# Vision tower kernel: two loads instead of six issued by ScalarE, and four products as three passes on rounded halves

## What is computed

```python
h = _L0_tok_ref(x, ...)                  # patches @ W_proj.T + b_proj + pos_emb
h = h + _L0_attn_ref(_layernorm(h), ...) # linear attention, 16 heads, feature map elu + 1, running sums
h = h + _L0_ffn_ref(_layernorm(h), ...)  # x @ base_w.T + base_b, plus softmax-gated low-rank experts
h = h + _L1_attn_ref(_layernorm(h), ...) # causal softmax attention, one head of width 256
h = h + _L1_ffn_ref(_layernorm(h), ...)  # sigmoid(xr @ W_r) * (relu(xk @ W_k)**2 @ W_v)
```

```python
result = jnp.einsum('bsd,od->bso', x, base_w) + base_b
logits = jnp.einsum('bsd,ed->bse', x, router_w) + router_b
mid = jnp.einsum('bsd,dr->bsr', x, lora_A)
...
scores = jnp.einsum('bqd,bkd->bqk', Q, K) / jnp.sqrt(jnp.asarray(d, x.dtype))
attn = jax.nn.softmax(scores, axis=-1)
return jnp.einsum('bqk,bkd->bqd', attn, V)
```

## Time and profile before

| | before |
|---|---|
| median of 3 runs | 196.55 us (195.1 to 197.55) |
| the profiled execution: time, span | 195.54 us, 193.5 us |
| PE busy | 178.7 us, 92% |
| PEld busy | 151.4 us, 78% |
| DVE busy | 144.4 us, 75% |
| ACT busy | 85.3 us, 44% |
| POOL busy | 84.3 us, 44% |

### The profile page before, as it was taken

One profiled execution on the slowest core, in us unless ns is written; L12 is line 12 of the kernel. 1 busy time (PEld: TensorE's weight loads), 2 busy tenths in 40 slices (PEclk: granted clock), 3 DMA queues, 4 the chain that ended last, 5 costly groups with the idle time before them and its releaser, 6 DMA issues.

```text
span 193.5 us, 4709 instructions
## 1 busy us (share of the span) xinstructions
PE 178.7 (92%) x1676; PEld 151.4 (78%) x1676; DVE 144.4 (75%) x471; ACT 85.3 (44%) x247; POOL 84.3 (44%) x144
## 2 busy tenths in 40 slices
...
GB/s 155 272 250 265 276 310 101 5 5 0 0 3 0 0 3 2 3 23 3 0 23 0 28 5 0 23 3 0 0 28 0 26 23 0 3 0 25 0 23 38
DMA packets 17201, 9.31 MB, mean 48 GB/s; under 512 B 11840, under 2 KB 17180, under 8 KB 17180
## 3 DMA queue, kind: packets, MB, share of 16 engines
...
q10 hardware_dynamic: 1448, 0.95, 1.8%
...
## 4 chain that ended last, share of the span: by engine, by line
PE 77%; SPq 9%; DVE 4%; ACT 2%; issue 2%; DMA 2%; POOL 1%; POOLq 0%; DVEq 0%; ACTq 0%
PE single L653 10%; PE quad L529 8%; PE single L529 7%; PE single L671 6%; PE single L738 5%; PE single L743 5%; PE quad L630 5%; PE single L700 5%; PE single L703 5%; PE single L644 5%; PE single L559 4%; SPq L314 4%; SPq L329 3%; PE single L727 3%; PE single L712 3%; PE single L688 3%
## 5 line engine op out<-in xcount | busy, mean ns | idle before, releaser
L429 POOL TENSOR_TENSOR ln_rs<-ln_ve,mhalf 108x1 f32<-108x1 f32 (+1 forms) x44 | 24.1, 549 | 50.2 <-DVE ln_ve L985 50.1
L1081 DVE TENSOR_TENSOR S<-quad,mask 108x864 f32<-108x864 f32 (+1 forms) x22 | 21.9, 1024 | 0.6 <-PE quad L630 0.6
L529 PE MATMUL single<-wp_hi,x_hi 128*108 128x256 f32 (+1 forms) x66 | 19.3, 293 | 2.0 <-DVE x_lo L939 2.0
L997 DVE TENSOR_SCALAR xn_back<-hB,ln_mv,ln_rs 108x256 f32<-108x256 f32 (+1 forms) x33 | 13.6, 412 | 7.4 <-POOL ln_rs L429 7.1
L529 PE MATMUL single<-wp_hi,x_lo 128*108 128x256 f32 (+1 forms) x66 | 18.5, 280 | 0.0
L529 PE MATMUL single<-wp_lo,x_hi 128*108 128x256 f32 (+1 forms) x66 | 18.5, 280 | 0.0
L442 POOL TENSOR_TENSOR x_lo<-xT,x_hi 128x648 fp32r<-128x648 f32 (+1 forms) x8 | 12.1, 1516 | 5.7 <-ACT x_hi L766 5.7
L457 POOL TENSOR_TENSOR hbb<-hB,baseb 108x256 f32<-108x256 f32 (+1 forms) x11 | 8.3, 753 | 14.2 <-DVE hB L1103 14.2
L971 DVE BATCH_NORM_STATS2 ln_st<-hB 108x6 f32<-108x256 f32 (+1 forms) x33 | 13.8, 422 | 0.3
L480 POOL TENSOR_TENSOR gated<-gated,hB 108x256 f32<-108x256 f32 (+1 forms) x11 | 8.4, 761 | 12.5 <-DVE gated L1183 12.5
L529 PEld LDWEIGHTS single<-wp_hi,x_hi 128*108 128x108 f32 (+1 forms) x66 | 11.2, 169 | 2.6 <-DVE wp_lo L934 2.1
...
## 6 DMA issues: line engine op xcount, KB each, us to landing
...
```

The source lines that it names most:

```text
L429: nc.gpsimd.tensor_tensor(L.rs[0:t, j:j + 1], L.ve[0:t, j:j + 1], mhalf[0:t, :], ALU.pow).then_inc(L.rstd_done, 1)
L529: ins = nc.tensor.matmul(out_ap, lhs, rhs, start=(start and n == 0), stop=(stop and n == len(terms) - 1))
L997: nc.vector.tensor_scalar(L.xn[0:t, j, :], h[0:t, i, :], L.mv[0:t, i, 0:1], L.rs[0:t, i:i + 1], ALU.subtract, ALU.mult).then_inc(L.xn_done, 1)
L1081: nc.vector.tensor_tensor(S[0:t, j, 2 * h:2 * h + 2, 0:4 * t].rearrange("p r (e t) -> p r e t", e=4), quad[0:t, 2 * h:2 * h + 2, 0:4 * t]. ...
```

## The change

1. ScalarE issues the two large loads only; the three of `pos` and the row of `b_proj` go to SyncE's queue, ahead of the three attention weights. `bv` and `bo` get semaphores of their own. `L1_attn_Vw` is loaded earlier, behind `cat` and ahead of units 6 and 7 of x.
2. The products of `ffn`, of `atv` (both) and of `sc` become `product3` on rounded halves. So the turned tokens are kept as `xn_hi` and `xn_lo`, `at` as `at_hi` and `at_lo`, and `wcat`, `G` and `L1_attn_Vw` as halves too. The new VectorE steps are `lo1`, `lo2` (one subtraction for each unit and norm), `lo3` (`at_low`, one for each unit), `late` (two for the weights) and `foldl`; the new ScalarE steps are `cat` and `vwh`.
3. Norm 1 is applied by ScalarE instead of VectorE (`VLN` is (2, 3)), with the GpSimd product `nb`.
4. `GROUPS` is [0,1], [2,3,4], [5,6,7], [8,9,10].
5. Buffers are shared: `kmin`, `qmin` with `kcum`, `qk`; `sm`, `probT` with `xr`; `gated` with `v1`; raw `wcat` and Vw with `S`; some small ones.
6. All five orders (but SyncE's own) and the banks are new. `router` now stands behind `hF.4` and `kf.0`.

The diff, without the order and bank tables and cut to what is told above:

```diff
-GROUPS = [[0, 1, 2], [3, 4, 5], [6, 7, 8], [9, 10]]
+GROUPS = [[0, 1], [2, 3, 4], [5, 6, 7], [8, 9, 10]]
-VLN = (1, 2, 3)
+VLN = (2, 3)
...
+        kmin, qmin = kcum, qk
...
+        wcat = staged[:, 0:KT * NCAT].rearrange("p (k n) -> p k n", k=KT)
+        vw_raw = staged[:, KT * NCAT:KT * (NCAT + E)].rearrange("p (k n) -> p k n", k=KT)
...
+        sm, probT = xr[0:TMAX, :, 0, :], xr[0:TMAX, :, 1, :]
+        gated = v1
...
             load_x(sp, 2)
+            for k in range(3):
+                sp.dma_start(pos[k * NTOK:(k + 1) * NTOK, :], a["L0_tok_pos_emb"]).then_inc(s["pos_loaded"], 16)
+            row(sp, bproj, "L0_tok_b_proj", "bproj_loaded")
...
-            load_w("L0_ffn_cat", wcat[:, :, :], s["cat_loaded"])
+            sp.wait_ge(s["wp_lo_ready"], 2)
+            load_w("L0_ffn_cat", wcat, s["cat_loaded"])
+            load_w("L1_attn_Vw", vw_raw, w_loaded["L1_attn_Vw"])
...
             def b_ffn(u):
...
-                pe.wait_ge(ln[1].xnT_ready, u + 1)
-                for k in range(KT):
-                    ins = nc.tensor.matmul(b[0:t, 0:NCAT], xnT_back[:, j, k, 0:t], wcat[:, k, :],
-                                           start=(k == 0), stop=(k == KT - 1))
-                ins.then_inc(s["ffn_mm"], 1)
+                pe.wait_ge(s["xn1_lo_ready"], u + 1)
+                product3(b[0:T[u], 0:NCAT], [(x, (cat_hi[:, k, :], cat_lo[:, k, :])) for k, x in enumerate(turned(u))]
+                         ).then_inc(s["ffn_mm"], 1)
...
             def b_atv(u):
...
+                pe.wait_ge(s["xn2_lo_ready"], u + 1)
+                x = turned(u)
                 for ft in range(KT):
...
+                    f = slice(ft * P, (ft + 1) * P)
+                    product3(b[:, ft * t:(ft + 1) * t], [((G_hi[:, k, f], G_lo[:, k, f]), x[k]) for k in range(KT)])
+                product3(b[0:t, E:2 * E], [(x[k], (vw_hi[:, k, :], vw_lo[:, k, :])) for k in range(KT)]
+                         ).then_inc(s["atv_mm"], 1)
...
             def b_sc(u):
...
-                pe.wait_ge(s["v1_ready"], u + 1)
...
+                pe.wait_ge(s["at_lo_ready"], u + 1)
+                product3(b[0:t, 0:t], [((at_hi[:, j, k, 0:t], at_lo[:, j, k, 0:t]), x) for k, x in enumerate(turned(u))]
+                         ).then_inc(s["sc_mm"], 1)
...
             load_x(act, 1)
-            for k in range(3):
-                act.dma_start(pos[k * NTOK:(k + 1) * NTOK, :], a["L0_tok_pos_emb"]).then_inc(s["pos_loaded"], 16)
-            row(act, bproj, "L0_tok_b_proj", "bproj_loaded")
...
+            def turned_low(n):
+                def step(u):
+                    j, t = u % UN, T[u]
+                    dve.wait_ge(ln[n].xnT_ready, u + 1)
+                    nc.vector.tensor_tensor(xn_lo[:, j, :, 0:t], tr(n, u), xn_hi[:, j, :, 0:t].bitcast(F32),
+                                            ALU.subtract).then_inc(s[f"xn{n}_lo_ready"], 1)
+                return step
+
+            def at_low(u):
+                j, t = u % UN, T[u]
+                dve.wait_ge(s["v1_ready"], u + 1)
+                nc.vector.tensor_tensor(at_lo[:, j, :, 0:t],
+                                        bank("atv", u)[:, 0:KT * t].rearrange("p (k t) -> p k t", k=KT),
+                                        at_hi[:, j, :, 0:t].bitcast(F32), ALU.subtract).then_inc(s["at_lo_ready"], 1)
```

More of the change, by code:

```diff
@@ L47 @@
 XLV = 3
-VLN = (1, 2, 3)
+VLN = (2, 3)
 BANKS = {
-    "fold": "2",
-    "tok": "01203320312",
-    "tr0": "31201110203",
-    "dc": "0320",
-    "av": "30220122030",
-    "wo": "21031220320",
-    "tr1": "20011000031",
-    "ffn": "32322312210",
-    "zt": "12101331223",
-    "lo": "30323131023",
-    "tr2": "33200013220",
-    "atv": "11030033122",
-    "sc": "10202133121",
-    "pt": "20113311032",
-    "pv": "13002233330",
-    "tr3": "01311220012",
-    "rk": "13112131313",
-    "ou": "10331011020",
+    "fold": "0",
+    "tok": "01202311013",
+    "tr0": "31130222311",
+    "dc": "2121",
+    "av": "33023120211",
+    "wo": "00312211002",
+    "tr1": "12330222131",
+    "ffn": "30300223321",
+    "zt": "10000033103",
+    "lo": "33213023102",
+    "tr2": "20303330211",
+    "atv": "22020003212",
+    "sc": "11331133302",
+    "pt": "22331310033",
+    "pv": "21321120332",
+    "tr3": "03102112131",
+    "rk": "01030220030",
+    "ou": "11330201212",
@@ L84 @@
-    zt.10 tr2.9 tr3.7 sc.8 lo.10 atv.9 pt.8 rk.7 pv.8 sc.9 tr2.10 ou.7 pt.9 atv.10 tr3.8 pv.9 sc.10 pt.10
-    pv.10 rk.8 tr3.9 tr3.10 ou.8 rk.9 rk.10 ou.9 ou.10
+    idle.20 tok.0 tok.1 tok.2 idle.4 tr0.0 idle.3 tok.3 tr0.1 tok.4 k.0 k.1 q.0 q.1 tok.5 fold.0 tr0.2 v.0 v.1
+    dc.0 tr0.3 s.0 tr0.4 tok.6 tr0.5 db.0 av.0 s.1 wo.0 tok.7 av.1 tr0.6 k.2 wo.1 tr1.0 k.3 q.2 ffn.0 tr0.7
+    q.3 tok.8 zt.0 tr1.1 v.2 lo.0 v.3 ffn.1 v.4 dc.1 s.2 tr2.0 tr0.8 tok.9 zt.1 atv.0 lo.1 db.1 av.2 sc.0 s.3
+    wo.2 pt.0 tr2.1 tr0.9 pv.0 tok.10 av.3 s.4 tr3.0 wo.3 tr1.2 atv.1 k.4 rk.0 sc.1 ffn.2 k.5 pt.1 ou.0 zt.2
@@ new lines @@
+    tr1.3 q.4 pv.1 lo.2 q.5 ffn.3 av.4 tr0.10 v.5 v.6 wo.4 tr3.1 zt.3 v.7 lo.3 tr2.2 dc.2 s.5 atv.2 rk.1 sc.2
+    tr2.3 s.6 ou.1 atv.3 pt.2 tr1.4 av.5 pv.2 av.6 db.2 ffn.4 sc.3 k.6 tr3.2 wo.5 pt.3 wo.6 zt.4 k.7 pv.3 lo.4
+    rk.2 tr1.5 q.6 q.7 ou.2 tr3.3 ffn.5 tr2.4 s.7 atv.4 dc.3 rk.3 tr1.6 zt.5 v.8 sc.4 ffn.6 ou.3 lo.5 pt.4 v.9
+    zt.6 pv.4 av.7 lo.6 v.10 tr2.5 wo.7 db.3 atv.5 tr3.4 tr2.6 s.8 sc.5 atv.6 tr1.7 pt.5 pv.5 sc.6 s.9 rk.4
+    pt.6 ffn.7 pv.6 tr3.5 ou.4 av.8 av.9 wo.8 rk.5 tr3.6 zt.7 wo.9 s.10 tr1.8 ou.5 lo.7 rk.6 ffn.8 av.10 ou.6
@@ L86 @@
+    wo.10 zt.8 tr1.9 tr2.7 lo.8 ffn.9 atv.7 tr1.10 zt.9 tr2.8 lo.9 sc.7 ffn.10 atv.8 pt.7 zt.10 tr2.9 pv.7
+    sc.8 lo.10 atv.9 pt.8 pv.8 tr3.7 sc.9 tr2.10 atv.10 pt.9 rk.7 tr3.8 pv.9 sc.10 ou.7 pt.10 pv.10 rk.8 tr3.9
+    tr3.10 ou.8 rk.9 rk.10 ou.9 ou.10
 """
 ACT_ORDER = """
[L88 to L90 removed]
```

208 lines of the change are left out of this document (104 added, 104 removed).

## The result

The change makes the kernel slower. The median of 4 runs is 202.88 us (201.74 to 204.99), against 195.82 us (193.72 to 197.55) for the kernel before in 4 runs on the same chip: a ratio of 1.038, with a 95% interval of 1.022 to 1.054, 7.1 us. The forecast was 201.5, within 196 to 206.

What follows compares the result with a forecast made beforehand. TensorE's steps bound the middle, the chain from engine to engine the ends. From 196.0 us, 3.6 + 1.3 + 0.8 - 0.5 + 0.3 = +5.5 us gave 201.5 us, range 196 to 206.

Steps and rivals of the forecast that it cites:

- Passes and first pass: TensorE in `ffn`, `atv`, `sc`: three rounded passes add 3.6 us; entering 33 new split steps adds 1.3 us.
- Passes cost by their columns: Rival, chance 0.1: the split steps on TensorE shrink to three quarters, -8.4 us, giving 189 to 190 us.
- VectorE, +0.8: Added subtractions ahead of `ffn`, `atv` and `sc` delay TensorE by 0.8 us, range 0 to 4; VectorE busy about 154.
- that rival (205 to 209): VectorE decides, chance 0.15: `_lo` steps come late in the middle, 8 us instead of 0.8, 205 to 209 us.
- The start, -0.5: First units: earlier table load, moved `router` and loads, wait before `tr0.1`; together -0.5 us, between -2.5 and +2.
- The end, +0.3: From 160 us on, `lo2` and `lo3` of the last units join the chain: 0 to 0.84 us, taken as 0.3.
- Half clock at the end: Gaps of TensorE near the end: longer ones could add 1 to 2 us, shorter save 1.4; no separate case.
- The middle stays full: Sign that the forecast is right: TensorE remains full in the middle, where it was busy 19.9 of 20 us.
- Won back at the ends: Rival, chance 0.25: new orders recover waits from 20 to 30 and 160 to 185 us, giving 196 to 199 us.

Runs made afterwards that it cites:

- the series: The change with rounded passes and plain products of several widths timed behind its last step; at 108 moving columns, three passes against two plain records: 0.336 to 0.224 us.
- the test of `lo3`: The change with the part of `atv` with G and `sc` plain, now also without the subtraction after `atv`: 195.63 us, ratio 1.0009 to the kernel before.
- the experiment with the norm: The change with norm 0 of unit 1 put ahead of x of unit 5 on ScalarE: 202.12 us, ratio 1.042 to the kernel before.

## Why the prediction was right, point by point

The forecast of 201.5 us and "slower" held, and so did the mechanism that carried it, narrow passes paced by their stationary side. Some of its terms were of another size, and the term for the start was made of parts that were wrong. Added up: the passes and their entry 4.9 us forecast, 5.0 measured; everything else +0.6 forecast, +1.6 measured at the same clock (6.6 less 5.0).

**Passes and first pass, +3.6 and +1.3.** Measured 4.8 us in the three steps (5.0 without the waits in the sums), for 4.9. By step, with 0.04 for the entry in each: `ffn` -0.13 forecast, -0.10 measured; `atv` +0.32 and +0.38; `sc` +0.26 and +0.15. The miss at `sc` was in the price before: I took 0.38 us from one row, while the median of the eleven steps is 0.465. The passes with G are 0.11 us apart, as a pass of 180 columns was in the earlier trace rows, and twelve take 1.35 us in the median, for 1.32 and an entry of 0.04: this price was right. The miss in `atv` is in the part with Vw, 0.755 us for 0.70. In the two units at 1.47 the second pass starts 0.24 us after the first, but the first starts only 0.03 us after the last plain record of 256 columns, so its interval holds time that belongs to that record; in the series, too, a change from plain to rounded costs nothing.

**Passes cost by their columns** (0.1): excluded by the rows and by the series. The Trainium skill, FP8 and Floating Point Precision, section TensorE Precision Notes, gives true FP32 four passes, from which I had worked out that three would be cheaper. Where the moving side has 108 columns, the trace does not agree with that; it does at 256, where a plain product is 0.432 us and three rounded passes are 0.360.

**VectorE, +0.8.** Its busy time is 154.4 us (forecast 154). Waits after `xn_lo` add up to 1.6 us, half of it at the end, and none is named after `at_lo`; without all subtractions the time is 1.6 us lower and the span 2.4. So the term was undersized, 0.8 for about 2, within the 0 to 4 kept for it, and by the test of `lo3`, made with the narrow products plain, it is `lo1` and `lo2` that cost. VectorE does not decide: that rival (205 to 209) is out.

**The start, -0.5.** The first pass comes 0.46 us sooner (forecast 0.6). ScalarE loads its table at 2.01 us, but then waits for the landing of the patch weight (timeline of ScalarE):

```profile
2.01 1.28 ACT L777 ACT_TABLE_LOAD   x1 [2.01 <-issue]
5.22 1.58 ACT L777 ACTIVATE wp_hi<-S 128x768 fp32r<-128x768 f32 x2 [1.93 <-DMA S<-in_L_tok_W_proj_dram]
...
21.10 0.74 ACT L777 ACTIVATE x_hi<-xT 128x648 fp32r<-128x648 f32 x1 [2.50 <-PE single L542]
```

TensorE stood before `tr0.1` as forecast, 1.39 us, at 22.48 us instead of 21.6:

```profile
22.48 0.38 PE L572 MATMUL single<-ident,xn_front 108*128 108x108 f32 x2 [1.39 <-ACT xn_front L824]
```

The reason given was right: that norm stands behind x of unit 5, and x of unit 5 waits for its DMA. The row of 21.10 us names TensorE as releaser, but that is `tok.3`, which ended at the same moment and for which ScalarE does not wait (see the experiment with the norm). What was off is the time: ScalarE takes x up at 21.10 us where it did at 20.20 before, with the loads in another order. The first 60 us together lose 5.8 us for 6.2 before, which looks like the gain of 0.5 that I forecast; but 0.5 us of it is filler, and the work done by 60 us is 0.2 us less. So **-0.5** was wrong by about 0.7 us, and its parts by more: `router` alone gains 1 us, the moved loads, which I had charged at nothing (0 to 1), cost 1.6 to 3 us in the kernel before, and removing the gap before `tr0.1` only moves it. That the errors nearly cancel is luck.

**The end, +0.3, and the middle.** Here the forecast was too low: 1.2 us more idle time from 160 us on (0.8 if the kernel before had kept full clock there, since its half clock shortened a wait by 0.4), and 1.2 in the middle; VectorE's 1.6 us of waits for `xn_lo` are part of both. The waits at the end are those for `xr` (0.50, 0.86, 0.41 us) and `xn_lo` (0.85), and one of 1.36 for a norm (`xn_back`), which other kernels at full clock show too. The gaps of the middle and of 30 to 60 us (28.66 of 30) come with the new orders: 28.65 with narrow products plain, 28.66 without subtractions, 29.90 with before's orders, even with three passes.

**Half clock at the end.** Forecast as a swing of 1 to 2 us, it can be larger. The clock did not fall in the profiled run, and in two of the four it did: 203.0 and 201.9 us at 0.983 against 198.8. Where the change was repeated it was less, 201.4 and 201.9 us at 0.980 and 0.982 against 200.5.

**The middle stays full:** 97.5 of 100 us, for 98.7. **Won back at the ends** (196 to 199): it was not. The router's wait of 1.88 us is gone, but 1.39 us before `tr0.1` stand in its place; of the 1.6 us of idle time that the first 30 us save, 0.5 is filler, 1.2 are lost again by 60 us and 1.2 at the end.
